# A transformer block on one Trainium2 core: the value fold in front, the score fold behind tile 0 as three fp32r products

## The chip, the cores and the metric

The kernel runs on one core of a Trainium2 chip. The metric is device time in microseconds (us), the median of the runs of a kernel. PE is TensorE, DVE is VectorE, ACT is ScalarE, POOL is GpSimd and SP is SyncE, which here only issues DMAs.

## The reference

Three layers, each with a residual; `x` is (16, 64, 512), the context (16, 1601, 512). fp32 throughout.

```python
def xattn(q, k, v, mask, gamma, beta):         # q = layernorm(x), k = v = ctx
    logits = einsum('bsd,btd->bst', q, k) / sqrt(512)
    attn = softmax(where(mask == 0, -9e15, logits))
    return layernorm(attn @ v) * gamma + beta
def attn(x, W_qkv, W_out):                     # x = layernorm(x), 64 tokens a sequence
    q, k, v = split(x @ W_qkv.T)
    return (softmax(q @ k.T / sqrt(512)) @ v) @ W_out.T
def ffn(x, router_w, expert_w1, expert_w2):    # x = layernorm(x), top 2 of 8 experts
    return sum_e gate_e * (gelu(x @ w1[e].T) @ w2[e].T)
```

## The kernel before, in words

The 1024 tokens are 8 tiles of 128 (two sequences each). One core runs five instruction streams, each written out in a fixed order and tied to the others by semaphores; there is no planner.

**Start.** The host gives the projection weights with the summed dimension on the partitions. They are turned on PE (`turn_pieces`, `turn_weights`, 128x128 transposes), copied out of PSUM, and folded in pairs: `m` is the product of query and key weights (the second layer's scores are xn m xn^T), `vo` the product of value and output weights. `fold` makes each as four 128x512 outputs of four fp32 matmuls. Each fp32 matmul shows as two PE instructions. The order is: 16 idle transposes (`keep_busy`) once the constants `cst` are there, turn wq and wk, fold `m`, tile 0's query and rest columns, tile 0's scores, turn wv, fold `vo`, tile 1's query. The result of `m` goes to `scores_w`; that of `vo` is split into two fp32r parts (`values_high` by ACT, `values_low` by DVE), for `values` multiplies fp32r parts three times (high by high, high by low, low by high).

**Turns.** In turn r (1 to 7) PE transposes the probabilities of tile r-1 (`turn_prob`), makes the scores of tile r in three blocks of 512 context rows and a rest of 65 (`scores`, L805; `rest_scores`), the second layer's keys of tile r-2 (`keys`, L861), then sums probabilities by context of tile r-1 (`sums`, L846: rest first, then three blocks), and between them the second layer's own scores, values, turned probabilities and output of tile r-2 (`own_scores` L871, `values` L879 to L881, `turn_own_probs` L887, `weigh` L893). DVE does masks and maxima (`softmax`), the low part of xn (`low_xn`, L1432), gates and ranks of the router, the next tile's query norm (`queries`), the own scores' maxima (`tops`, L1421), and the other norms. ACT does exponentials and copies. POOL turns the mask into bounds (`bounds`, L619, one 128x1601 pass a tile) and adds the bias (`add_bias`, L625).

**Loads.** All context loads go through SP's one DMA queue. The context is loaded twice, as rows (`load_ctx`, L497) and turned (`load_turned`, L510), 1 MiB a piece, into one buffer for each block: SP waits until PE has used the block of the tile before, and then issues the next. A turn loads 12 MiB, a mask and the rest rows.

**After the last turn** come the last sums, the second layer of tiles 6 and 7, the router, and the gather of expert 0's rows (`first_rows`, `hot_rows` L930), with the first weight blocks of the expert layer split into fp32r parts (`split_high` by ACT L1202, `split_low` by DVE L1501). `keep_busy` (L938) puts idle transposes where PE would wait. Then eight experts run (`up` L1066 to L1068, `down` L1095 to L1097), the second product two chunks behind the first; the last expert has two token tiles, whose rows are scaled by DVE (`gate`, L1669) and added to the output by indirect DMAs of POOL (L707).

Of the kernel before, what the change touches and what calls it, by code (L numbers as in the profile page):

```python
# [70 lines left out]
def fill_order():  # L71

    for which in ("wq", "wk", "m"):
        for n in range(KC):
            yield which, 0, n
    for kind in ("xq", "rest0", "rest1", "qr"):
        yield kind, 0, 0
    for which in ("wv", "vo"):
        for n in range(KC):
            yield which, 0, n  # L80
    for kind in ("xq", "rest0", "rest1"):
        yield kind, 1, 0
    for r in range(1, TILES):
# [20 lines left out]
def by_act(kind, t, n):  # L104
    if kind == "xn":
        return t != LAST
    return n % 2 == 0 if kind in ("wq", "wk", "m") else kind not in ("vo", "out", "qr", "logit", "rank", "pt")
# [15 lines left out]
def bank_at(kind, t, n=0):  # L123
    if kind == "wk":
        return n
# [104 lines left out]
def build(nc, x, ctx_in, ctx_turned, mask, gamma, beta, w_qkv, w_out, w_router, w1, w2, consts, acc):  # L230
# [5 lines left out]
    with ExitStack() as stack:  # L236
# [26 lines left out]
        with (nc.sbuf_tensor("before_low2", [P, 44680], F32), nc.sbuf_tensor("values_low2", [P, 2, D], F32R) as values_low2):  # L263
            pass
        high_c = sb("high_c", [P, 2, WBLK], F32R)
# [56 lines left out]
        turned_q, turned_k = [view(21504 + i * WBLK, KC, D) for i in range(2)]  # L322
        turned_v = turned_q
# [74 lines left out]
        cst_in, gb_in = sem("cst_in"), sem("gb_in")  # L398
        wq_in, wk_in = [[sem(f"{name}_in{k}") for k in range(KC)] for name in ("wq", "wk")]
        vo_high, xn_high, xn_split = sem("vo_high"), sem("xn_high"), sem("xn_split")  # L400
        wv_in, wo_in, rw_in = sem("wv_in"), sem("wo_in"), sem("rw_in")
# [88 lines left out]
        def _(sp):  # L490
# [44 lines left out]
            sp.dma_start(raw_v, w_qkv[:, 2 * WBLK:].rearrange("p (k h) -> p k h", k=KC)).then_inc(wv_in, 16)  # L535
            sp.dma_start(raw_out, w_out.rearrange("p (k h) -> p k h", k=KC)).then_inc(wo_in, 16)
# [9 lines left out]
            sp.wait_ge(filled, filled_at("vo", 0, KC - 1))  # L546
# [63 lines left out]
        def _(pool):  # L610
# [84 lines left out]
            gather(STATIC[0], 3)  # L695
            for t in range(LAST - 1, TILES):
# [45 lines left out]
        def _(pe):  # L742
# [19 lines left out]
            def turn_weights(kind, raw, hc):  # L762
                o = open_fill(kind, 0, hc)
                for k in range(KC):
                    mm = pe.transpose(o[:, k * P:(k + 1) * P], raw[:, k, hc * P:(hc + 1) * P], ident)
                mm.then_inc(filled, 1)

            def fold(kind, left, right):
# [985 lines left out]
```

## Time and profile before

| | us |
|---|---|
| median of 3 runs | 768.01 (766.83 to 769.06) |
| the profiled execution | 767.6 |
| its span | 765.9 |
| PE busy | 736.6 (96%) |
| DVE / ACT / POOL busy | 443.4 / 309.5 / 153.9 |

The span is the time from the first to the last instruction. A busy share is an average over stages with different limits; what an edit is worth is read from its own stage. In rows of the timeline an engine's idle time before an instruction stands in brackets with what ended it. A line such as L479 or L780 can be that of a helper.

### The profile page before, as it was taken

The page shows a single profiled execution, that of the slowest core. Times are in us where ns is not written, and L with a number is a line of the kernel's source. Part 1 is how long each engine was busy: PE and PEld are TensorE (multiplying, and loading weights), DVE is VectorE, ACT ScalarE, POOL GpSimd, SP SyncE. Part 2 cuts the span into 40 slices and gives each one's busy share as a digit, 9 for nine tenths or more (in the row PEclk, how much of TensorE's full clock was granted, in tenths as well). Part 3 has the DMA queues.
Part 4 walks back from the last instruction along what each step waited for, and adds up shares of the span by engine and source line. Part 5 has one row for each costly group of instructions (what it writes and reads, how often), then busy time and mean ns, then how long its engine had stood idle before and what let it go on. Part 6 is the DMA issues. An engine that isn't in the chain of part 4 may idle for free.

```text
span 765.9 us, 12386 instructions
## 1 busy us (share of the span) xinstructions
PE 736.6 (96%) x4794; PEld 560.5 (73%) x4794; DVE 443.4 (58%) x1005; ACT 309.5 (40%) x518; POOL 153.9 (20%) x162
## 2 busy tenths in 40 slices
PE   6999999999999999999999999999999999999992
PEld 5444455454545554578999999999998998888882
DVE  5243467676767664886775545555556556555620
ACT  2022212121223221335555555565555666666620
POOL 2132130404132200132310210310211230120201
PEclk9999999999999999999999999999999999999997
DMA  9999999999999999921545545655657565665302
GB/s 328 408 419 418 398 402 418 397 419 402 418 403 417 400 416 398 330 63 32 202 165 196 143 151 194 160 193 179 185 192 199 198 227 193 214 207 216 86 1 28
DMA packets 36333, 199.40 MB, mean 260 GB/s; under 512 B 4700, under 2 KB 5100, under 8 KB 15536
## 3 DMA queue, kind: packets, MB, share of 16 engines
q1 hardware_dynamic: 29912, 186.74, 63.2%
q0 software_dynamic: 4704, 9.14, 6.4%
q10 hardware_dynamic: 1656, 2.70, 1.0%
q8 instruction: 40, 0.66, 0.3%
q14 instruction: 21, 0.17, 0.1%
HBM read 188.19 MB, written 10.37 MB: 259 GB/s over the span
## 4 chain that ended last, share of the span: by engine, by line
PE 82%; DVE 11%; issue 2%; ACT 2%; DMA 1%; POOL 0%; DVEq 0%; POOLq 0%; ACTq 0%
PE ps L805 11%; PE ps L1066 8%; PE ps L1068 8%; PE ps L1067 8%; PE ps L846 7%; PE ps L1088 4%; PE ps L1089 4%; PE ps L1090 4%; PE ps L1095 4%; PE ps L1096 4%; PE ps L1097 4%; PE ps L773 4%; DVE xn_parts L1432 2%; PE ps L826 2%; PE ps L780 1%
## 5 line engine op out<-in xcount | busy, mean ns | idle before, releaser
L479 POOL TENSOR_TENSOR small<-small 128x1 f32<-128x1 f32 x64 | 24.1, 377 | 556.3 <-DVE yb_space L1669 197.4
L1068 PE MATMUL ps<-xT,low_a 128*128 128x288 f32 (+5 forms) x384 | 110.1, 287 | 0.0
L1274 ACT ACTIVATE hid<-ps 128x288 f32<-128x288 f32 (+5 forms) x128 | 50.6, 396 | 143.7 <-PE ps L1068 141.1
L1638 DVE TENSOR_TENSOR h_ring<-hid,h_ring 128x288 fp32r<-128x288 f32 (+5 forms) x128 | 55.7, 436 | 86.1 <-ACT h_ring L1279 86.0
L1501 DVE TENSOR_TENSOR low_a<-w_raw_a,high_b 128x2048 fp32r<-128x2048 f32 x32 | 73.4, 2292 | 39.2 <-ACT high_b L1202 39.2
L846 PE MATMUL ps<-arena 128*64 128x512 f32 (+1 forms) x416 | 94.1, 597 | 0.8 <-DVE arena L1401 0.8
L805 PE MATMUL ps<-arena 128*64 128x512 f32 x384 | 85.5, 596 | 0.2 <-ACT arena L1149 0.2
L1142 ACT COPY arena<-ps 128x512 f32<-128x512 f32 (+2 forms) x89 | 41.4, 525 | 100.6 <-PE ps L780 61.3
L1066 PE MATMUL ps<-xT,high_b 128*128 128x288 f32 (+5 forms) x256 | 74.9, 292 | 0.0
L1067 PE MATMUL ps<-xT,high_b 128*128 128x288 f32 (+5 forms) x256 | 73.4, 287 | 0.0
L1068 PEld LDWEIGHTS ps<-xT,low_a 128*128 128x128 f32 x384 | 72.4, 189 | 0.0
L846 PEld LDWEIGHTS ps<-arena 128*64 128x64 f32 (+1 forms) x416 | 27.9, 136 | 54.1 <-issue 51.8
L805 PEld LDWEIGHTS ps<-arena 128*64 128x64 f32 x384 | 26.3, 137 | 48.5 <-issue 47.8
L1202 ACT CAST high_b<-w_raw_a 128x2048 fp32r<-128x2048 f32 x32 | 60.8, 1904 | 0.0
L1090 PE MATMUL ps<-h_ring,low_a 128*128 128x288 f32 (+2 forms) x192 | 56.9, 296 | 0.0
L1279 ACT CAST h_ring<-hid 128x288 fp32r<-128x288 f32 (+5 forms) x128 | 53.4, 418 | 4.1
L1066 PEld LDWEIGHTS ps<-xT,high_b 128*128 128x128 f32 x256 | 48.3, 189 | 1.4
L1067 PEld LDWEIGHTS ps<-xT,high_b 128*128 128x128 f32 x256 | 48.3, 189 | 1.1
L1501 DVE TENSOR_TENSOR low_b<-w_raw_b,high_c 128x2048 fp32r<-128x2048 f32 x16 | 36.7, 2293 | 20.6 <-ACT high_c L1202 20.5
L1501 DVE TENSOR_TENSOR low_a<-w_raw_a,high_a 128x2048 fp32r<-128x2048 f32 x16 | 36.6, 2292 | 19.9 <-ACT high_a L1202 19.9
L619 POOL TENSOR_SCALAR arena<-arena 128x1601 f32<-128x1601 int32 x8 | 45.0, 5624 | 0.0
L1377 DVE SCALAR_TENSOR_TENSOR arena<-arena,ps 128x1024 f32<-128x1024 f32 (+1 forms) x16 | 15.3, 956 | 44.8 <-PE ps L805 44.8
(217 smaller groups left out, 1644.7 us busy)
## 6 DMA issues: line engine op xcount, KB each, us to landing
arena<-in_ctx_turned SPq DMA_DIRECT2D x48, 1024.0 KB, 20.4
arena<-in_ctx SPq DMA_DIRECT2D x48, 1024.0 KB, 18.7
w_raw_a<-in_w SPq DMA_DIRECT2D x48, 1024.0 KB, 4.8
w_raw_b<-in_w SPq DMA_DIRECT2D x16, 1024.0 KB, 4.8
arena<-in_mask SPq DMA_DIRECT2D x8, 800.5 KB, 22.1
tokens_x<-arena SPq DMA_DIRECT2D x11, 256.0 KB, 12.4
arena<-in_w_qkv SPq DMA_DIRECT2D x8, 256.0 KB, 4.8
out<-res SPq DMA_DIRECT2D x8, 256.0 KB, 9.2
```

Source lines behind the costliest of these rows:

```text
L619: pool.tensor_scalar(bound, mask_sb, 0, MASKED - LIMIT, ALU.is_equal, ALU.mult).then_inc(bound_ready, 1)
L805: mm = pe.matmul(bank(blk)[64 * b:64 * b + 64, :], xqT[:, k, 64 * b:64 * b + 64], ctxT[blk][:, b, k, :], start=(k == 0), stop=(k == KC - 1))
L846: mm = pe.matmul(att_ps[64 * b:64 * b + 64, :], probT[0:m, c, 64 * b:64 * b + 64], rows, start=(n == 0 and c == chunks[0]), stop=(n == NBL ...
L1066: pe.matmul(o, w_high[2 * f][:, cols], high[:, k, 0:w.width], start=(k == 0), stop=False)
L1067: pe.matmul(o, w_high[2 * f][:, cols], low[:, k, 0:w.width], start=False, stop=False)
L1068: mm = pe.matmul(o, w_low[2 * f][:, cols], high[:, k, 0:w.width], start=False, stop=(k == KC - 1))
L1090: mm = pe.matmul(o, low[:, cols], h_high[:, 0:w.width], start=False, stop=final)
L1202: act.copy(w_high[j], w_raw[j]).then_inc(w_high_ready, 1)
L1274: nc.scalar.activation(hid[:, c % 2, 0:w.width], bank(c % UP_BANKS)[:, 0:w.width], ACT.Gelu).then_inc(gelu_done, 1)
L1279: act.copy(h_ring[:, c % RING, 0, 0:w.width], hid[:, c % 2, 0:w.width]).then_inc(h_high_ready, 1)
L1501: dve.tensor_tensor(w_low[j], w_raw[j], w_high[j].bitcast(F32), ALU.subtract).then_inc(w_ready, 1)
L1638: dve.tensor_tensor(h_ring[:, c % RING, 1, 0:w.width], hid[:, c % 2, 0:w.width], h_ring[:, c % RING, 0, 0:w.width].bitcast(F32), ALU.subtr ...
```

## The change

It moves and rewrites several things at once. (1) The value and output weights are loaded, turned and folded first; the identity is loaded alone, ahead of the other constants. (2) The query and key weights are turned after that, kept as fp32r parts (high by ACT, low by DVE), and folded behind tile 0's scores and tile 1's query as 48 fp32r matmuls. (3) In the turns the second layer's own scores, values and turned probabilities of tile r-2 stand behind the rest sum alone, not behind the first block too, the output product one block earlier, and DVE takes `tops` ahead of `queries`. (4) After the last turn the low part of weight block 1 goes from DVE to POOL, and `low_xn` stands ahead of the last `attended`. (5) 23 idle transposes stand ahead of the last `ranks`, where 18 stood, and 5 more behind it. (6) The last three `down` chunks of the last expert run tile by tile.

```diff
 def fill_order():
-    for which in ("wq", "wk", "m"):
+    for which in ("wv", "vo", "wq", "wk"):
...
+    for n in range(KC):
+        yield "m", 0, n
     for r in range(1, TILES):
...
-            for raw, first, here in ((raw_q, 0, wq_in), (raw_k, KC, wk_in)):
+            for raw, of, first, here in ((raw_v, w_qkv, 2 * KC, wv_in), (raw_out, w_out, 0, wo_in), (raw_q, w_qkv, 0, wq_in),
+                                         (raw_k, w_qkv, KC, wk_in)):
                 for k in range(KC):
-                    sp.dma_start(raw[:, k, :], w_qkv[:, (first + k) * D:(first + k + 1) * D]).then_inc(here[k], 16)
-            sp.dma_start(res[:, 0:D], x[0:P, :]).then_inc(x_in, 16)
+                    sp.dma_start(raw[:, k, :], of[:, (first + k) * D:(first + k + 1) * D]).then_inc(here[k], 16)
+                if raw is raw_out:
+                    sp.dma_start(res[:, 0:D], x[0:P, :]).then_inc(x_in, 16)
...
-            sp.dma_start(raw_v, w_qkv[:, 2 * WBLK:].rearrange("p (k h) -> p k h", k=KC)).then_inc(wv_in, 16)
-            sp.dma_start(raw_out, w_out.rearrange("p (k h) -> p k h", k=KC)).then_inc(wo_in, 16)
...
-            sp.wait_ge(filled, filled_at("vo", 0, KC - 1))
+            sp.wait_ge(filled, filled_at("m", 0, KC - 1))
...
             gather(STATIC[0], 3)
+            pool.wait_ge(w_high_ready, 2)
+            pool.wait_ge(w_ready, 1)
+            carry_pool_waits(pool, own)
+            pool.tensor_tensor(w_low[1], w_raw[1], w_high[1].bitcast(F32), ALU.subtract).then_inc(w_ready, 1)
...
+            def fold_scores():
+                wait_copied(pe, "wk", 0, KC - 1)
+                for m in range(KC):
+                    o = open_fill("m", 0, m)
+                    cols = slice(m * P, (m + 1) * P)
+                    for hc in range(KC):
+                        pe.matmul(o, high_q[:, hc, cols], high_k[:, hc, :], start=(hc == 0), stop=False)
+                        pe.matmul(o, high_q[:, hc, cols], low_k[:, hc, :], start=False, stop=False)
+                        mm = pe.matmul(o, low_q[:, hc, cols], high_k[:, hc, :], start=False, stop=(hc == KC - 1))
                     mm.then_inc(filled, 1)
...
-            pe.wait_ge(cst_in, 16)
-            keep_busy(16, bank(0))
+            pe.wait_ge(id_in, 16)
+            keep_busy(6, bank(0))
+            turn_pieces("wv", raw_v, wv_in)
+            fold_values()
             turn_pieces("wq", raw_q, wq_in)
+            wait_copied(pe, "vo", 0, KC - 1)
             turn_pieces("wk", raw_k, wk_in)
-            for n in range(KC - 2, KC):
-                wait_copied(pe, "wk", 0, n)
-            fold("m", turned_q, turned_k)
             turn_query(0)
             turn_rest(0)
+            wait_copied(pe, "wq", 0, KC - 1)
             for blk in range(NBLK - 1):
                 scores(0, blk)
             rest_scores(0)
-            pe.wait_ge(wv_in, 16)
-            for hc in range(KC):
-                turn_weights("wv", raw_v, hc)
-            pe.wait_ge(wo_in, 16)
-            wait_copied(pe, "wv", 0, KC - 1)
-            fold("vo", turned_v, raw_out)
             turn_query(1)
             turn_rest(1)
+            fold_scores()
+            pe.wait_ge(cst_in, 16)
...
                 sums(r - 1, PV_ORDER[0])
-                sums(r - 1, PV_ORDER[1])
                 if runs(r - 2):
                     own_scores(r - 2)
                     values(r - 2)
                     turn_own_probs(r - 2)
-                sums(r - 1, PV_ORDER[2])
+                sums(r - 1, PV_ORDER[1])
                 if runs(r - 2):
                     weigh(r - 2)
+                sums(r - 1, PV_ORDER[2])
                 sums(r - 1, PV_ORDER[3])
...
-            keep_busy(18, open_fill("rank", LAST))
+            keep_busy(23, open_fill("rank", LAST))
             ranks(LAST)
+            wait_copied(pe, "logit", LAST)
+            keep_busy(5, bank(bank_at("logit", LAST)))
             hot_rows(LAST)
...
                     up(w, c)
-                    if c >= LAG:
+                    if w.kind == EXPERTS - 1 and c == FC - 1:
+                        for t in range(2):
+                            for late in range(FC - 1 - LAG, FC):
+                                down(w, late, t)
+                    elif c >= LAG:
                         down(w, c - LAG)
...
+                if runs(r - 2):
+                    tops(r - 2)
                 if runs(r + 1):
                     queries(r + 1)
                 if runs(r - 2):
-                    tops(r - 2)
                     copy_pt(r - 2)
                     second_norm(r - 2)
...
-            for j in range(2):
-                split_low(STATIC[0], j)
+            split_low(STATIC[0], 0)
             gates(LAST - 2)
             route_second(LAST - 2)
+            low_xn(LAST - 1)
             attended(LAST)
-            low_xn(LAST - 1)
```

## Rows read from the trace of the kernel before

**Rows 1.** Busy time by stretch: us, each engine (instructions), granted clock, DMA share, GB/s.

```profile
192.20:228.70 36.50, 36.34 (x226) 19.04 (x225) 25.00 (x87) 8.25 (x19) 9.56 (x8) 1.00 1.02 410
```

**Rows 2.** The chain that ended last, in the start: start us, us, what.

```profile
14.31 13.97 PE ps L773 x32
...
29.41 10.52 PE ps L805 x48
...
58.64 1.37 PE ps L826 x10
```

**Rows 3.** The same chain, one fp32r product of 512 columns.

```profile
290.03 0.23 PE ps L880
```

**Rows 4.** Line L529, the eight 256 KiB weight pieces.

```profile
L529 SPq DMA_DIRECT2D arena<-in_w_qkv x8: 399/432/505, 0.9 to 4.3; - x8
...
DMA to landing us min/median/max: 3.8/4.8/5.9
```

**Rows 5.** Line L510, the last turned blocks of tile 0.

```profile
L510 SPq DMA_DIRECT2D arena<-in_ctx_turned x2: 522/523/524, 8.8 to 9.4; - x2
...
DMA to landing us min/median/max: 20.3/21.6/22.8
```

**Rows 6.** Line L510, the last turned blocks of tile 3.

```profile
L510 SPq DMA_DIRECT2D arena<-in_ctx_turned x3: 1866/1880/2157, 95.4 to 99.2; - x3
...
DMA to landing us min/median/max: 27.3/27.4/28.9
```

**Rows 7.** PE's timeline: tile 3's third score block, then turn 5.

```profile
129.08 3.65 PE L805 MATMUL ps<-arena 128*64 128x512 f32 x16
...
211.65 4.51 PE L846 MATMUL ps<-arena 65*64 65x512 f32 x20
215.99 0.64 PE L871 MATMUL ps<-arena 128*64 128x64 f32 x16
...
219.76 0.33 PE L887 MATMUL ps<-cst,own_space 128*128 128x128 f32 x1 [0.16 <-ACT own_space L1183]
```

**Rows 8.** DVE's timeline in the same turn.

```profile
209.94 2.93 DVE L1432 TENSOR_TENSOR xn_parts<-arena,xn_parts 128x512 fp32r<-128x512 f32 x1
...
215.25 0.69 DVE L1350 BATCH_NORM_STATS2 small<-res 128x6 f32<-128x512 f32 x1
...
218.20 0.47 DVE L1421 TENSOR_REDUCE small<-ps 64x1 f32<-64x64 f32 x2
```

**Rows 9.** POOL's timeline in the same turn.

```profile
208.19 5.63 POOL L619 TENSOR_SCALAR arena<-arena 128x1601 f32<-128x1601 int32 x1
...
218.95 1.28 POOL L625 TENSOR_TENSOR res<-res,arena 128x512 f32<-128x512 f32 x1
```

**Rows 10.** DVE's timeline after the last turn.

```profile
312.34 4.49 DVE L1501 TENSOR_TENSOR low_a<-w_raw_a,high_a 128x2048 fp32r<-128x2048 f32 x2 [1.05 <-ACT high_a L1202]
...
332.69 0.69 DVE L1432 TENSOR_TENSOR xn_parts<-arena,xn_parts 128x512 fp32r<-128x512 f32 x1
```

**Rows 11.** POOL's timeline, the last of the three gathers.

```profile
332.97 1.17 POOL L672 DMA_INDIRECT rows_space<-tokens_x,route  x1
```

**Rows 12.** PE's timeline ahead of the expert layer.

```profile
342.77 2.21 PE L930 MATMUL ps<-arena 128*128 128x288 f32 x8
...
349.98 0.39 PE L912 MATMUL ps<-route,cst 128*128 128x8 f32 x2 [0.75 <-DVE route L1466]
...
351.25 3.66 PE L930 MATMUL ps<-arena 128*128 128x288 f32 x8 [0.66 <-DVE arena L1496]
```

**Rows 13.** Busy time by stretch, columns as in rows 1.

```profile
352.00:353.00 1.00, 1.00 (x4) 0.70 (x3) 0.90 (x5) 0.40 (x1) 0.19 (x1) 0.50 0.00 0
```

**Rows 14.** The timeline of the end.

```profile
751.60 1.46 DVE L1669 TENSOR_SCALAR yb_space<-ps,route 128x512 f32<-128x512 f32 x2 [2.24 <-PE ps L1097]
...
753.24 1.57 POOL L707 DMA_INDIRECT out<-yb_space,route  x1 [0.47 <-POOL small L479]
...
755.19 1.48 POOL L707 DMA_INDIRECT out<-yb_space,route  x1 [0.16 <-issue]
```

More of the change, by code:

```diff
@@ L106, in by_act @@
         return t != LAST
-    return n % 2 == 0 if kind in ("wq", "wk", "m") else kind not in ("vo", "out", "qr", "logit", "rank", "pt")
+    return n % 2 == 0 if kind in ("wv", "m") else kind not in ("wq", "wk", "vo", "out", "qr", "logit", "rank", "pt")
 ACTS = [by_act(kind, t, n) for kind, t, n in FILLS]
@@ L123, in bank_at @@
 def bank_at(kind, t, n=0):
[L124 removed]
+    if kind == "wq":
         return n
@@ L1093, in down @@
                     for t, (a, m) in enumerate(w.tiles):
+                        if only is not None and t != only:
+                            continue
                         o = bank(y_bank(w, t))[0:m, :]
@@ L1119, in _ @@
                     more = in_use(pe)
-            for c in range(FC - LAG, FC):
-                down(STATIC[-1], c)
             with pe.If(more > 0):
@@ L1223, in _ @@
                 act.copy(values_high[:, n, :], bank(bank_at("vo", 0, n))).then_inc(vo_high, 1)
-            copy_query(1)
-            copy_rest(1)
+            for kind, dst in (("wq", high_q), ("wk", high_k)):
+                for n in range(KC):
+                    act.wait_ge(filled, filled_at(kind, 0, n))
+                    act.copy(dst[:, n, :], bank(bank_at(kind, 0, n))).then_inc(turned_high, 1)
+            for p in range(2):
+                copy_query(p)
+                copy_rest(p)
+            exps(0)
+            for n in range(0, KC, 2):
+                copy_fill("m", 0, scores_w[:, n, :], n)
             act.wait_ge(zero_out, 16)
@@ L1511, in _ @@
             own.then_next(dve.memset(cum[0], 0.0))
+            for n in range(1, KC, 2):
+                copy_fill("wv", n, turned_v[:, n, :])
+            queries(0)
             dve.wait_ge(cst_in, 16)
@@ L1516, in _ @@
                 own.then_next(dve.memset(capacity[:, p:p + 1], float(WIDTHS[p])))
-            for kind, dst in (("wq", turned_q), ("wk", turned_k)):
-                for n in range(1, KC, 2):
-                    copy_fill(kind, n, dst[:, n, :])
-            queries(0)
-            for n in range(1, KC, 2):
-                copy_fill("m", n, scores_w[:, n, :])
-            softmax(0)
-            queries(1)
             for n in range(KC):
@@ L1528, in _ @@
                                   ).then_inc(copied[False], 1)
+            for which, (kind, high, part) in enumerate((("wq", high_q, low_q), ("wk", high_k, low_k))):
+                dve.wait_ge(filled, filled_at(kind, 0, KC - 1))
+                for n in range(KC):
+                    dve.wait_ge(turned_high, which * KC + n + 1)
+                    dve.tensor_tensor(part[:, n, :], bank(bank_at(kind, 0, n)), high[:, n, :].bitcast(F32), ALU.subtract
+                                      ).then_inc(copied[False], 1)
+            queries(1)
+            softmax(0)
+            for n in range(1, KC, 2):
+                copy_fill("m", n, scores_w[:, n, :])
             for r in range(1, TILES):
```

58 lines of the change are left out of this document (27 added, 31 removed).

## The prediction

> **What bounds the kernel now.** I read the busy times by stretch first. In a steady turn PE is busy for 36.34 of 36.50 us at full granted clock, and in the same row the DMA engines are full as well: share 1.00, 410 GB/s [rows 1]. So two resources stand near their limit at once. A turn's loads are 12 MiB of context (12.58 MB), a mask (0.82 MB), rest rows (0.27 MB) and a token store (0.26 MB), 13.9 MB; at 410 GB/s that is 34.0 us against PE's 36.5. PE sets the pace, and the queue catches up some 2.5 us a turn. What matters is how late the queue is at the beginning. I then read the chain of waits of the start: a fold is 13.97 us on PE, tile 0's scores run from 29.41 to 39.93, and turn 1 begins at 58.64 [rows 2]. No DMA stands in the chain after the first 5 us, so a reader could think that loads are hidden. The landing times say how thinly. Tile 3's last turned piece is issued at 99.2 and lands 28.9 us later, at 128.1 [rows 6]; PE takes that block at 129.08 [rows 7]. The slack is 1.0 us, the least that I found in turns 1 to 7. Third, I read one turn on PE, DVE and POOL side by side [rows 7 to 9], and last the stretch between the turns and the expert layer [rows 10 to 13] and the end [rows 14].
>
> **The start.** The score fold goes from 32 instructions in 13.97 us [rows 2] to 48 of 0.232 us (0.23 in [rows 3]), 11.15 us: 2.8 us less PE work. The new order in time: the value weights need 16 transposes, not 32, ahead of the first fold, and 6 idle ones, not 16. Pieces land from 4.7 us on, one each 0.78 us (4.7 to 10.2 for eight) [rows 4], so the value fold can begin at about 8.4 and ends 14.0 later, at 22.4. Turning wq and wk takes about 4.6, to 27.0. The parts are made by ACT and DVE bank by bank; DVE's subtraction is 0.69 each [rows 10], and tile 0's columns need the banks of wk, so I give PE 3 us of waiting, to 30.3. Here the queue speaks: all sixteen pieces now stand ahead of the context. Tile 0's last turned piece lands at 9.4 + 22.8 = 32.2 now [rows 5]; eight more pieces of 0.78 put it at 38.5. The third block would be wanted at 37.4, so scores end at 38.5 + 3.5 = 42.0. Rest, tile 1's query and rest take 1.6, the fold 11.2: turn 1 begins at 54.8, **3.8 us earlier** than 58.64.
>
> Does it last? The bytes ahead of tile 3's last piece are the same before and after, in nearly the same order, and the queue never runs empty in either. Then that piece lands at 128.1 whatever PE does, and PE, which wanted it at 129.08, can be at most 1.0 us earlier there. The value and output weights go from two 1 MiB transfers to eight small ones: eight at 0.78 are 6.3 us, 2.1 MB at 410 GB/s 5.1, so the queue may be 0 to 1.2 us later. I take 0.4, since the 0.78 is from the first microseconds, when the queue has hardly begun. That leaves **-0.6**, with -1.0 and +0.2 as bounds. If the queue is no bound, the bounds are -3.8 and, with no wait for tile 0's third block, -4.9.
>
> **The turns.** PE has the same instructions in another order. What counts is when the turned own probabilities (L887) can go. Now PE does the rest sum (4 of the 20 instructions from 211.65, 0.87 us), the first block (3.5), own scores from 215.99 to 216.56, values for 2.9, and is ready at 219.44; L887 starts at 219.76, 0.32 late [rows 7]. It waits for the exponentials, 1.56 us after DVE begins `tops` at 218.20 [rows 8]. After the change PE begins own scores at 211.65 + 0.87 = 212.5 and is ready at 216.0. DVE is at the queries at 215.25 [rows 8], which is where `tops` now stands; it can't be earlier, for low_xn takes 2.93 us there (0.69 when alone [rows 10]), beside POOL's bounds of 208.19 to 213.82 [rows 9]. So L887 starts at 215.25 + 1.56 = 216.8, 0.84 late. Taking the first block away from behind the own work costs 3.5 us of cover and `tops` gives back 2.95: **+0.5 us a turn**. That holds for turns 4, 5 and 6, +1.55. In turn 3 POOL's mask lands late, the wait is 1.5 to 1.9 us now, and the same count gives 1.35: -0.5. Turn 2 is level (-0.1), and in turn 7 POOL has no bounds, low_xn is short and nobody waits. Sum **+0.95**, between 0 (if low_xn gets in ahead of POOL) and +1.6. Behind `tops` queries delay copy_pt by 3 us, but the first block's 3.5 us cover that. The output product one block earlier gives second_norm 4 us more; in turn 7 this is the only one that shows, 0.2, counted below.
>
> **After the last turn.** DVE's two subtractions are 4.49 us [rows 10]; one goes, 2.25 us off DVE. The last `attended` waits for PE's sums anyway from about 0.8 us ahead of its start, and low_xn ahead of it takes 0.7 off a wait of PE's, so of 2.25 about 0.7 reaches PE. POOL takes the subtraction up behind the last gather (332.97 + 1.17 now [rows 11]), about 332 then, since gates are also 2.25 earlier. Its price isn't in the trace: 2048 columns at L625's 1.28/512 are 5.1 us, at L619's 5.63/1601 7.2 us [rows 9]; I take 5.1, a tensor_tensor like L625. It meets tile 7's low_xn (332.69 now, 332.0 then [rows 10]) and the routing of tile 6 on DVE. low_xn beside POOL took 2.2 us longer than alone [rows 8, 10]. Bounds: -0.7 if DVE isn't held, +0.8 if low_xn and the routing behind it are held as in rows 8. I take **-0.3**, as most of DVE's work there is on a few columns or from PSUM. The Trainium skill ("SBUF — State Buffer", "Who interferes with whom") has a DVE instruction with two SBUF inputs fully blocked by a POOL instruction that reads SBUF. By it the whole 5.1 us would be closed to low_xn, and the term would be positive; the 2.93 us in rows 8 agrees with it in kind, though there DVE was free 0.95 us ahead of POOL's shown end.
>
> **The clock.** PE idles for 0.75 us ahead of the ranks and 0.66 behind them, and the eight fp32 instructions that follow take 3.66 us; the same eight took 2.21 at 342.77 [rows 12]. The granted clock at 352 to 353 is 0.50, that is 1.2 GHz and not 2.4 [rows 13]. The new transposes fill both gaps: five at 0.12 are 0.6 of the 0.75 and 0.6 of the 0.66, and delay nothing. With the clock kept PE saves 1.45; behind it DVE's four splits of about 0.5, which start only once the gates are done, keep 0.3 of that: **-1.1** (bounds 0 and -1.5).
>
> **The end.** Of the last 18 products (0.232 each) the first tile's last is number 15 now and number 9 then. That is 1.4 us, less 0.1 for the last chunk's parts, which come later than PE asks. The first scaling moves from 751.60 to 750.3, and POOL's first DMA from 753.24 to 751.95. The second is now 1.95 behind the first, at 755.19 [rows 14]; then it needs tile 2's rows (752.3, plus 0.73 and 0.91 to the DMA) at 753.95: **-1.2** (bounds -0.9 and -1.4).
>
> **Sum.** -0.6 + 0.95 - 0.3 - 1.1 - 1.2 = -2.25 us. The profiled execution took 767.6, so 765.3 by the sum; it lies 0.4 under the median of 768.0, which gives 765.7. A measurement of this kernel can tell about 0.3%, 2.3 us: my forecast stands on that bound.
>
> **Rivals.**
> - *The queue is no bound.* For it: no DMA in the chain, slack of 4 us and more from turn 4 on. Against: 1.00 share and 1.0 us of slack in turn 3. The 3.8 us reach the end: 768.0 - 2.25 - 3.2 = 762.5. Chance 0.15.
> - *The clock falls all the same,* since 0.15 us gaps and small transposes may not count as work. 766.8. Chance 0.11.
> - *The turns pay more:* 1.6 for the turns and the queue 1.0 later, so that the front gives nothing: 768.0 - 2.25 + 0.65 + 0.6 = 767.0. Chance 0.13.
> - *The turns pay nothing:* 764.7. Chance 0.05.
> - *Slower.* POOL's subtraction holds DVE's low_xn of tile 7 to its end. At 7.2 us it ends at 339.2, low_xn at 339.9, values start 5.4 us later than 334.5 and the tail is +4.7 in place of -0.3: 770.7. It decides from a delay of PE of some 2.6 us on. For it: the stretched low_xn. Against: DVE may come first, by 0.1 us. Chance 0.10.
> - The forecast, 765.7 with its own range of 764.3 to 767.1: chance 0.46, 0.25 of it under 765.7.
>
> Faster by over 0.3%: 0.25 + 0.15 + 0.05 = 0.45. Within: 0.21 + 0.11 + 0.13 = 0.45. Slower by over 0.3%: 0.10. The range of 762.4 to 768.6 leaves out the slow case and some of the wide ends.
>
> **What would show it.** Turn 1's first transposes at about 55; a wait for a turned piece at tile 2's or tile 3's third score block, which isn't in the chain now; tile 3's third block at 128.1 to 128.9; 0.8 us ahead of L887 in turns 4 to 6; one POOL subtraction of 5 us from 332 on, and a long low_xn or routing step beside it; granted clock 1.0 at 350 to 356; the second output DMA 1.2 us nearer to the first. If tile 3's block starts at 126 or earlier, the cap by the queue was wrong, and most of my working with it.

## The result, and the profile after

The changed kernel takes **778.65 us** (median of 4 runs, 772.72 to 779.44) against 767.42 for the kernel before beside it: ratio 1.0127, 95% interval 1.0074 to 1.0181. It is slower by 11 us where I had forecast 2.25 less, and it lies outside my range. The profiled execution took 779.44 us, with a span of 777.8 (765.9 before).

Read by checkpoints, the 11.8 us between the two profiled executions arise in two places. The last turn's transposes of probabilities begin at 306.6 instead of 301.7, 4.9 late. From there to the expert layer's first product it is 62.4 us instead of 54.3 (369.0 less 306.6, 356.0 less 301.7), another 8.1. The expert layer is as long as it was, and behind it 1.3 us are won.

**The start.** First the chain of waits (start us, us, what). In the kernel before it had no DMA behind the first 5 us:

```profile
16.14 25.50 DMA arena<-in_ctx_turned
41.68 5.35 PE ps L822 x16
...
104.25 28.65 DMA arena<-in_ctx_turned
132.94 3.68 PE ps L822 x16
```

The two DMA lines answer to [rows 5, 6]. Tile 0's last turned piece lands at 41.6, not at 32.2 as before or at 38.5 as I had it, and tile 3's at 132.9, not at 128.1. PE takes them the moment they land. Its timeline in tile 0, with the idle time and its releaser in brackets:

```profile
28.46 0.63 PE L797 MATMUL ps<-cst,arena 128*128 128x128 f32 x4 [1.89 <-DVE fold_low L1549]
...
35.83 3.65 PE L822 MATMUL ps<-arena 128*64 128x512 f32 x16 [2.06 <-DMA arena<-in_ctx_turned]
41.68 1.84 PE L822 MATMUL ps<-arena 128*64 128x512 f32 x4 [2.20 <-DMA arena<-in_ctx_turned]
```

Turn 1 begins at 59.4, 0.8 later than before and 4.6 later than my 54.8. The piece's landing is 3.1 of the 4.6. Another 1.7 is TensorE's clock. Behind the waits of 2.06 and 2.20 us the granted clock is 0.50 from 41.9 to 45.3, and the third block takes 5.35 us, where such a block takes 3.65 at other times:

```profile
40.00:45.00 5.00, 3.32 (x8) 0.92 (x10) 1.22 (x1) 0.00 (x0) 0.00 (x0) 0.69 1.01 374
```

The queue never ran empty, yet it moved less. Busy time by stretch (here and above with the columns of [rows 1]) of the kernel after and then of the kernel before:

```profile
15.00:20.00 5.00, 5.00 (x13) 2.18 (x12) 2.08 (x12) 0.90 (x2) 0.00 (x0) 1.00 1.06 337
20.00:25.00 5.00, 5.00 (x28) 3.27 (x27) 1.38 (x2) 1.32 (x3) 0.00 (x0) 1.00 1.02 346
```

```profile
15.00:20.00 5.00, 5.00 (x13) 2.13 (x13) 4.72 (x9) 0.59 (x1) 5.00 (x1) 1.00 1.02 416
20.00:25.00 5.00, 5.00 (x13) 2.25 (x12) 1.41 (x2) 0.11 (x1) 0.43 (x1) 1.00 1.02 410
```

The DMA share stands above 1.00 in all four rows, but the bytes went from 416 and 410 GB/s to 337 and 346.

**The turns.** Turn 5 takes 37.00 us instead of 36.50 [rows 1], and L904, which is L887 of before, waits 0.60 instead of 0.16 [rows 7]:

```profile
197.46:234.46 37.00, 36.40 (x227) 19.05 (x225) 25.11 (x87) 8.29 (x20) 9.54 (x8) 1.00 1.01 407
```

```profile
221.13 0.33 PE L904 MATMUL ps<-cst,own_space 128*128 128x128 f32 x1 [0.60 <-ACT own_space L1203]
```

**After the last turn.** POOL, DVE and PE side by side in the profiled execution:

```profile
338.18 4.51 POOL L703 TENSOR_TENSOR low_a<-w_raw_a,high_a 128x2048 fp32r<-128x2048 f32 x1
```

```profile
337.75 4.97 DVE L1363 SCALAR_TENSOR_TENSOR small<-small 128x1 f32<-128x1 f32 x1
342.75 0.16 DVE L1365 SCALAR_TENSOR_TENSOR small<-small 128x1 f32<-128x1 f32 x1
```

```profile
334.87 3.84 PE L878 MATMUL ps<-arena 128*128 128x128 f32 x32
343.55 1.12 PE L797 MATMUL ps<-cst,arena 128*128 128x128 f32 x4 [4.84 <-DVE arena L1379]
...
347.95 0.63 PE L897 MATMUL ps<-values_low,xn_parts 128*128 128x512 f32 x1
348.38 0.63 PE L898 MATMUL ps<-values_high,xn_parts 128*128 128x512 f32 x1
```

```profile
342.30:352.30 10.00, 8.75 (x40) 7.24 (x41) 4.92 (x22) 1.59 (x6) 0.54 (x2) 0.50 0.14 52
```

A DVE step on one column, 0.22 us at other times, takes 4.97. It ends at 342.72, and POOL's subtraction at 342.69. PE, which waits for that normalization, is idle for 4.84 us. From 342.2 on, still within the idle time, its granted clock is 0.50, that is 1.2 GHz, for 10.2 us, and the value products start 0.43 us apart instead of 0.23. A further stretch at half clock, of 3.4 us at 311.5, also follows a wait of PE's (0.94 us).

The other executions of the changed kernel bear the clock out: the three at 778.5 to 779.4 us have a mean granted clock of 0.983 over the whole, the one at 772.7 has 0.990, like the profiled execution of the kernel before.

**Clock and end.** These two steps worked as forecast. The eight instructions behind the last ranks take 2.21 us, not 3.66 [rows 12], and the second output DMA starts 1.9 us behind PE's last product (765.1), where it was 3.3 [rows 14]:

```profile
365.74 2.21 PE L947 MATMUL ps<-arena 128*128 128x288 f32 x8
```

```profile
763.44 0.75 DVE L1696 TENSOR_SCALAR yb_space<-ps,route 128x512 f32<-128x512 f32 x1 [1.05 <-PE ps L1115]
...
765.08 1.57 POOL L715 DMA_INDIRECT out<-yb_space,route  x1 [0.47 <-POOL small L483]
...
767.03 1.48 POOL L715 DMA_INDIRECT out<-yb_space,route  x1 [0.16 <-issue]
```

### The profile page after: what moved, and what is told of

Same layout as the page of the kernel before. It is cut to its first block, busy times and chain, and to the rows that moved or that the text cites. A ratio compares the mean times of both kernels' runs of the same rounds, so it can differ in the third digit from the quotient of the medians.

```text
span 777.8 us, 12441 instructions
## 1 busy us (share of the span) xinstructions
PE 739.7 (95%) x4810; PEld 564.8 (73%) x4810; DVE 442.5 (57%) x1010; ACT 310.5 (40%) x520; POOL 158.5 (20%) x164
## 4 chain that ended last, share of the span: by engine, by line
PE 78%; DVE 7%; DMA 7%; SPq 4%; issue 1%; ACT 1%; POOL 0%; DVEq 0%; POOLq 0%; ACTq 0%
PE ps L863 10%; PE ps L1082 8%; PE ps L1084 8%; PE ps L1083 8%; PE ps L822 8%; DMA arena<-in_ctx_turned 7%; PE ps L1104 4%; PE ps L1105 4%; PE ps L1106 4%; PE ps L1113 4%; PE ps L1114 4%; PE ps L1115 4%; SPq L514 2%; PE ps L797 1%; DVE xn_parts L1453 1%
## 5 line engine op out<-in xcount | busy, mean ns | idle before, releaser
L863 PE MATMUL ps<-arena 128*64 128x512 f32 (+1 forms) x416 | 96.0, 606 | 1.4 <-DVE arena L1422 0.9
L822 PE MATMUL ps<-arena 128*64 128x512 f32 x384 | 87.8, 606 | 6.0 <-DMA arena<-in_ctx_turned 5.8
L1162 ACT COPY arena<-ps 128x512 f32<-128x512 f32 (+2 forms) x83 | 38.4, 519 | 97.3 <-PE ps L797 70.5
L822 PEld LDWEIGHTS ps<-arena 128*64 128x64 f32 x384 | 26.7, 138 | 56.5 <-issue 47.1
L1522 DVE TENSOR_TENSOR low_a<-w_raw_a,high_a 128x2048 fp32r<-128x2048 f32 x15 | 34.4, 2293 | 19.9 <-ACT high_a L1222 19.9
## 6 DMA issues: line engine op xcount, KB each, us to landing
tokens_x<-arena SPq DMA_DIRECT2D x11, 256.0 KB, 11.8
```

Of the source, the lines that this page charges most:

```text
L822: mm = pe.matmul(bank(blk)[64 * b:64 * b + 64, :], xqT[:, k, 64 * b:64 * b + 64], ctxT[blk][:, b, k, :], start=(k == 0), stop=(k == KC - 1))
L863: mm = pe.matmul(att_ps[64 * b:64 * b + 64, :], probT[0:m, c, 64 * b:64 * b + 64], rows, start=(n == 0 and c == chunks[0]), stop=(n == NBL ...
L1522: dve.tensor_tensor(w_low[j], w_raw[j], w_high[j].bitcast(F32), ALU.subtract).then_inc(w_ready, 1)
```

## The experiments

My theory after reading the two traces had two parts: POOL's subtraction shuts DVE out (and PE's clock pays for the idle time), and the load queue, later than I took it to be, undoes the new start. The rivals were that the new start costs PE time of its own, and that the loss after the last turn is only a follow-up of a later start and other turns. Each run stands against the kernel before timed beside it, whose median was between 767.08 and 767.74.

| part of the change | us | ratio, interval | my term |
|---|---|---|---|
| start alone | 769.29 | 1.0023, 1.0003 to 1.0044 | -0.6 |
| turns alone | 769.27 | 1.0033, 1.0021 to 1.0045 | +0.95 |
| last turn alone (POOL's subtraction, low_xn first) | 771.76 | 1.0070, 1.0047 to 1.0094 | -0.3 |
| clock and end alone | 765.51 | 0.9982, 0.9970 to 0.9994 | -2.3 |
| all but POOL's subtraction | 768.62 | 1.0024, 1.0014 to 1.0035 | |

The four parts add up to 1.08% (0.23 + 0.33 + 0.70 - 0.18), within the interval of the whole.

**All but POOL's subtraction.** DVE does both blocks again:

```diff
-            pool.tensor_tensor(w_low[1], w_raw[1], w_high[1].bitcast(F32), ALU.subtract).then_inc(w_ready, 1)
...
-            split_low(STATIC[0], 0)
+            for j in range(2):
+                split_low(STATIC[0], j)
```

> The changed kernel with one part undone: DVE makes the low part of weight block 1 again, POOL does not; low_xn stays ahead of the last attended. Theory 'port': POOL's 4.5 us subtraction held one small DVE step for 4.97 us, PE idled 4.84 us behind it and its clock was at half for the 10.24 us after; without it both go, and the time falls by 6 to 8 us to about 771.5, with no DVE step over 1.5 us in that stretch and granted clock 1.0 there. Rival 'late tail': the tail is slow because the queue and the turns made everything late, and the order around low_xn costs; then the time stays at 777 to 779 and PE still has a wait of some 5 us. In either case tile 3's third score block still starts at about 132.9, 3.9 us later than in the kernel before.

768.62 (768.02 to 769.97 over 10 runs). The one instruction is worth 10 us in the changed kernel by the medians (of 4 executions with it and 10 without), and without it the executions lie within 2 us of each other instead of 7.

**Wide pieces.** The changed kernel with wq and wk as one 1 MiB transfer each, rows of 8 KiB in place of 2 KiB:

```diff
+                if raw is raw_q or raw is raw_k:
+                    sp.dma_start(raw, of[:, first * D:(first + KC) * D].rearrange("p (k h) -> p k h", k=KC)).then_inc(here[0], 16)
+                    continue
```

> The changed kernel, but the query and key weights come as one 1 MiB transfer each (rows of 8 KiB) in place of four of 256 KiB (rows of 2 KiB). Theory 'row size': the eight extra small pieces with 2 KiB rows put the load queue 4.1 us late by the end of tile 0's loads (44.1 against 40.0) and 4.8 at tile 3; with wide rows the queue is 2 to 4 us earlier and tile 3's third score block starts at 129.5 to 131 and not at 132.9, so the time falls by 2 to 3.5 us. Rival 'order': the queue is late because of when the identity, the constants and the small loads of ACT's queue mix with SP's; then landing times move by less than 1 us and the time by less than 1.

770.56 (767.90 to 775.83), POOL's subtraction still in it, so the median says little of the queue. The page's line on packets of the changed kernel and of this run (36333 packets in the kernel before):

```profile
DMA packets 37341, 199.40 MB, mean 256 GB/s; under 512 B 4812, under 2 KB 5468, under 8 KB 16800
```

```profile
DMA packets 36478, 199.40 MB, mean 260 GB/s; under 512 B 4717, under 2 KB 5373, under 8 KB 15681
```

A good yardstick of the queue's lateness is the landing of the slots' write, which stands behind all the first loads: 40.0 in the kernel before, 44.1 after, 41.5 here. It varies from one execution to the next, though. In the ten traces with the old start it is 39.7 to 41.2, in the five with the new start and small pieces 42.2 to 44.1, and with wide pieces 41.5 and 43.0 (the second from a run further on). So wide pieces give back some 1 us on the average of so few, and most of the lateness has another cause. Tile 3's third block is at 130.3 here, as the theory had it, but at 131.3 and 133.3 in two further runs with wide pieces, and at 131.4 to 132.9 with small ones.

**Clock and end alone**, on the kernel before (the transposes and the order of the last 18 products, as in the diff of the change).

> The kernel before with two parts of the change alone: the 5 + 5 more idle transposes around the last ranks, and the last expert's last down chunks tile by tile. My sum gave -1.1 and -1.2: 765.1 against 767.4, ratio 0.997. The granted clock should stay 1.0 at 352 to 355, and the second output DMA should start 1.2 us nearer to the end of PE's work. Rival: a clock that falls all the same leaves -1.2 (0.9984); if the end is set by the DMAs' landing and not by their issue, less.

765.51 against 767.08. The profiled execution shows 2.8 less (764.84 against 767.6), no half clock ahead of the expert layer, and its first product 1.5 earlier. The timed median keeps 1.6 of it. The traces of all the runs show most of the reason: in the ten without this edit, the eight instructions behind the last ranks take 2.92 to 3.90 us in five and 2.21 in the other five; in the nine with it they always take 2.21. So the loss was there in half of these executions only, and 3.66 against 2.21, from which I priced the edit, was one of those. The mean of the ten is 2.80, which makes it worth 0.6 us and not 1.45.

**Turns alone**, PE's and DVE's order as in the change, on the kernel before.

> The kernel before with the order of the turns alone: own scores, values and turned probabilities behind the rest sum, the output product one block earlier, tops ahead of queries. Theory: 0.5 us a turn lost in turns 4 to 6, 0.5 won in turn 3, in sum +1.0 us (ratio 1.0013), and turns of 36.96 us in place of 36.50. Rival: the earlier second_norm wins that back after the last turn, ratio 1.000; or the changed meeting of DVE and POOL costs more, 1.003.

769.27: dearer than my +0.95, by the interval +1.6 to +3.5. The turns are 36.96 us, 0.46 longer, as in the whole.

**The start alone.** Value fold first, score fold in fp32r parts, everything behind as before.

> The kernel before with the new start alone: value fold first, score fold as 48 products of fp32r parts behind tile 0's scores; turns, last turn, clock and end as before. Queue theory: turn 1 begins some 3 us earlier (about 56), but tile 3's third score block comes 2 to 3 us later than before's 129.1, and the time is 1.5 to 2.5 us over the kernel before (about +0.3%). Rival (the delay of the start is not the queue's but that of the parts made by ACT and DVE): turn 1 begins at 58 or later. My prediction on record had -0.6 for this part.

769.29. Turn 1 begins at 56.5, 2.2 earlier than in the kernel before, and tile 3's third score block at 132.4, 3.4 later. Between them PE waits above all 2.99 us for plain context and 0.66 for a turned piece:

```profile
80.44 1.94 PE L859 MATMUL ps<-arena 128*64 128x512 f32 x8 [2.99 <-DMA arena<-in_ctx]
```

So the score fold's gain was there, and the queue took more than all of it. The granted clock is 1.00 from the start to turn 3 in this trace, so here the loss isn't the clock's. The clock can come on top, though: of the eight traces of kernels with the new start and the full queue, seven have one or two stretches of about 3.4 us or more at half clock before 90 us, and none of the nine with the old start and the full queue has one. What these stretches cost in the end was not measured.

**The same with the queue relieved.** If the queue takes it, then taking load off the queue must give it back. Both kernels get the same edit, which halves tile 1's turned context:

```diff
+                    n = KC // 2 if p == 1 else KC
-                    sp.dma_start(ctxT[blk][:, b, :, :], ctx_turned[2 * p + b, :, LOADED_TURNED - 1 - blk, :, :]
+                    sp.dma_start(ctxT[blk][:, b, 0:n, :], ctx_turned[2 * p + b, :, LOADED_TURNED - 1 - blk, 0:n, :]
```

> The kernel before, but tile 1's turned context is loaded by half (3.1 MB less ahead of everything from tile 1 on; what stands in the buffers is used in place of the other half, so the numbers that it computes are others; PE's work is the same). It is the base line for the next run. Both theories: within 0.5 us of the kernel before, since no PE wait for a load of more than 0.6 us is in its trace.

> The new start alone, with tile 1's turned context loaded by half, as in the run beside it (the same loads left out). Queue theory: with 7 us of transfers taken away the gain at turn 1 reaches the end, so the time is 2.5 to 3.5 us UNDER that of the relieved kernel before, where the start alone without relief is 1.5 to 2.5 over. Rival (the new start costs PE time of its own, or clock): the relieved pair differs by about as much as the unrelieved one, +1.5 to +2.5.

The kernel before went to 765.64 (0.9971, 0.9957 to 0.9986), the one with the new start to 764.57 (0.9953, 0.9933 to 0.9973). The new start costs 1.6 us with the full queue and saves 1.1 with the relieved one. The saving by itself isn't clear of the noise, for the two intervals overlap. The swing of 2.7 us between the pairs is: I estimate its standard error from the single executions at 0.9. The rival, which excludes a swing, is out. But I had expected a saving of 2.5 to 3.5, and the trace tells why it is less. At tile 3's third block the new start is 1.1 ahead (127.0 against 128.1). In the same turn L901 (L887 of before) begins at 144.5 in both, behind a wait of 1.26 us with the new start and of none in the other:

```profile
144.48 0.33 PE L901 MATMUL ps<-cst,own_space 128*128 128x128 f32 x1 [1.26 <-ACT own_space L1197]
```

POOL's bounds of this turn, which need a mask from the same queue, run from 133.0 to 138.6 in both (the mask lands at 132.7 with the new start and POOL takes it at once; in the other it lands at 131.0 and POOL waits for DVE), and DVE's low_xn beside them ends at 137.6 in both, however early it began. It takes 4.09 us in the one and 2.92 in the other:

```profile
132.98 5.62 POOL L624 TENSOR_SCALAR arena<-arena 128x1601 f32<-128x1601 int32 x1
```

```profile
133.55 4.09 DVE L1447 TENSOR_TENSOR xn_parts<-arena,xn_parts 128x512 fp32r<-128x512 f32 x1
```

That is a second way from the queue to PE: mask, POOL's bounds, DVE, tops, exponentials, L887. The relieved kernel before, too, was to be level and gained 2.1 us, although no wait of PE's over 0.6 us for a load stood in its trace: its L887 in turn 3 lost its wait of 1.48, and the mask, on which POOL had waited, lands at 131.0 instead of 135.0.

**The last turn alone.** POOL's subtraction and low_xn ahead of the last attended, on the kernel before.

> The kernel before with the last turn's part of the change alone: POOL makes the second static block's low parts (one subtraction of 2048 columns), DVE's low_xn ahead of the last attended. Theory (DVE's small steps of the router, with operands in SBUF, are shut out for as long as POOL's instruction runs, and PE's idle time then brings its clock down): 3 to 10 us slower, single times spread over 5 us and more, since it depends on which of the two comes first; in the trace one small DVE instruction of 2.5 to 5 us beside POOL's. Rival (the loss after the last turn comes only together with the later start and the new order of the turns): within 1 us of the kernel before. My prediction had -0.3.

771.76 (768.96 to 777.70). The single executions are of two kinds: three at 777.3 to 777.7 with a mean granted clock of 0.983 or 0.984, the others at 769.0 to 772.8 with 0.986 to 0.992. The profiled execution is the fastest of them (768.96), and even there DVE's step ends with POOL's, at 337.57 and 337.54:

```profile
332.96 4.58 POOL L699 TENSOR_TENSOR low_a<-w_raw_a,high_a 128x2048 fp32r<-128x2048 f32 x1
```

```profile
334.40 3.17 DVE L1460 SCALAR_TENSOR_TENSOR route<-route,cst 128x8 f32<-128x8 f32 x1
```

The rival, that the loss needs the rest of the change, is out. The edit has low_xn in front as well; on another version that alone changed nothing (further on), so the loss is POOL's subtraction.

**A quarter of it.** POOL makes 512 of the 2048 columns. In the first form DVE's own share stood ahead of the first block and waited 2.85 us for ACT's parts, a fault of my edit; the second form keeps the old order.

```diff
-            pool.tensor_tensor(w_low[1], w_raw[1], w_high[1].bitcast(F32), ALU.subtract).then_inc(w_ready, 1)
+            pool.tensor_tensor(w_low[1][:, 0:BLK], w_raw[1][:, 0:BLK], w_high[1][:, 0:BLK].bitcast(F32), ALU.subtract).then_inc(w_ready, 1)
```

> The same with POOL doing 512 of the 2048 columns (DVE the other 1536, ahead of it, where it did all of them before). Theory of the hold: the longest that DVE can be held falls from 4.5 us to about 1.2, PE's idle time stays under a microsecond more than before, and the time is within 1 us of the kernel before (it may even be under it by 0.7, what DVE saves). Rival (what costs is the handing over, POOL's start and the semaphores between the engines, and not the length): as slow as the full one.

> The kernel before with POOL making 512 of the 2048 columns and low_xn first, and DVE's share in the old order (the first block as soon as its high parts are there). Theory (the time is lost by DVE being shut out for the length of one POOL instruction, 1.27 us here): within 1 us of the kernel before, and the runs within 3 us of each other. Rival (it is the meeting of the two engines, whatever its length, or the handing over): some 2 us slower and spread over 8, as the first quarter run.

The first form took 769.66 (ratio 1.0026, 1.0002 to 1.0050; 765.82 to 774.62), 2.3 over the kernel before where I had expected 1 at most, the second 768.02 (1.0015, 0.9995 to 1.0035). POOL's instruction is 1.28 us in it. Eleven of the twelve runs are between 764.9 and 769.7, and one is 774.57. So handing the work over costs little: 4.4 us for 2048 columns, 0.6 for 512, which is within the noise. Neither trace has a held step, however. In the second form POOL's 1.28 us run from 334.32, DVE waits for PE from 334.29 on and then, at 335.10, takes up a step that reads PSUM. So the short instruction met nothing, and what a meeting with it costs isn't shown. The spread did not go away quite as expected; the one at 774.57 has a mean granted clock of 0.984, the others 0.989 and over.

**Whole, but in four instructions.**

```diff
+            for q in range(4):
+                cols = slice(q * BLK, (q + 1) * BLK)
+                part = pool.tensor_tensor(w_low[1][:, cols], w_raw[1][:, cols], w_high[1][:, cols].bitcast(F32), ALU.subtract)
+            part.then_inc(w_ready, 1)
```

> The kernel before with POOL's whole subtraction, low_xn first, but as four instructions of 512 columns. If DVE's step gets in between two POOL instructions, no DVE step is longer than about 1.4 us, several are long, and the time is 0 to 2 us over the kernel before, with runs of 777 gone. If POOL keeps what they share over all four, there is a step of 2.5 to 5 us as with one instruction, and the time is again near 771 with runs of 777.

771.40 (1.0065, 1.0043 to 1.0087), as dear as in one. DVE, whose step is shown as beginning 0.09 us ahead of the first of the four, did not get in between them:

```profile
333.24 4.99 POOL L701 TENSOR_TENSOR low_a<-w_raw_a,high_a 128x512 fp32r<-128x512 f32 x4
```

```profile
332.55 0.69 DVE L1439 TENSOR_TENSOR xn_parts<-arena,xn_parts 128x512 fp32r<-128x512 f32 x1
333.15 5.25 DVE L1568 CAST arena<-arena 128x288 f32<-128x288 int32 x1
338.44 0.48 DVE L1428 TENSOR_REDUCE small<-ps 64x1 f32<-64x64 f32 x2
```

**The changed kernel once more**, a single execution with its profile.

> The changed kernel as it is, for a second look. Theory: a DVE step of up to 5 us beside POOL's subtraction, PE idle for some 5 us behind it and its clock at half for 10 us, if the time is near 779; if it is near 772, the long step is shorter or falls where PE still has work, and the clock stays up.

771.67. The held step is another one, a comparison on 8 columns of 2.57 us, ending at 341.26 with POOL's 341.23:

```profile
338.69 2.57 DVE L1477 SCALAR_TENSOR_TENSOR route<-route,cst 128x8 f32<-128x8 f32 x1
```

PE still had its value products to do and was idle for 2.12 us only, and half clock lasted 3.4 us instead of 10. So which of DVE's steps POOL meets, and what PE has left to do then, most likely makes the difference between 772 and 779; it rests on one trace of each kind.

**Better versions.** On DVE tops go ahead of the queries, PE keeps the turn of before, and clock and end are as changed:

```diff
+                if runs(r - 2):
+                    tops(r - 2)
                 if runs(r + 1):
                     queries(r + 1)
                 if runs(r - 2):
-                    tops(r - 2)
                     copy_pt(r - 2)
```

> The kernel before with three things of the change alone: on DVE tops go ahead of the queries (PE's order of the turn stays that of before), the transposes around the last ranks, and the end with the first tile's products first. The transposes and the end alone gave 765.5 against 767.1. Theory of the turns (the order on DVE gives, the order on PE takes cover away): L887's wait of 0.3 us goes in each of five turns, and the time is 1 to 2 us under those two alone, 764. Rival: the queries now delay what is behind them, and nothing is gained or 0.5 lost: 765.5 to 766.

**762.86** (0.9939, 0.9917 to 0.9960), 4.9 us under the kernel before, 1.6 of it the clock and the end, and so some 3.3 DVE's order. In the trace it is 2.7 us less from L887 of turn 2 to that of turn 7. The steady turn is 36.12 us, with PE busy for all of it:

```profile
190.50:226.62 36.12, 36.12 (x226) 19.02 (x225) 24.95 (x87) 8.23 (x20) 9.55 (x8) 1.00 1.02 410
```

```profile
216.55 0.40 PE L881 MATMUL ps<-values_high,xn_parts 128*128 128x512 f32 x1
216.78 0.27 PE L887 MATMUL ps<-cst,own_space 128*128 128x128 f32 x1
```

> The best kernel so far (tops first on DVE, transposes around the ranks, the end; 762.9 against 767.7), and low_xn ahead of the last attended. Theory: it takes 0.7 off a wait of PE's after the last turn, 762.2. Rival: attended is on the path as well and the two cancel, 762.9.

> The changed kernel without POOL's subtraction and with PE's order in the turn as before, and wq and wk loaded as 1 MiB each. So it is the best kernel with the new start added (and low_xn first). Queue theory: the new start costs 0.5 to 1.5 us with the wide loads, so 763.3 to 764.5. Rival (with shorter turns PE is closer to the queue, and a late queue costs more): 765 and over.

low_xn first gives 762.78 (0.9928, 0.9909 to 0.9947), the same. With the new start and wide loads added it is 764.26 (0.9951, 0.9932 to 0.9970), 1.5 more, timed beside it, as the queue theory had it.

**ACT's loads later.** In the kernels with the new start, x's second block, gamma, beta and the router's weights go from 9 us on, beside the pieces of wq and wk. On the start alone, and on the version just before this, they were moved:

```diff
-            act.dma_start(res[:, D:2 * D], x[P:2 * P, :]).then_inc(x1_in, 16)
...
                     act.copy(dst[:, n, :], bank(bank_at(kind, 0, n))).then_inc(turned_high, 1)
+            act.dma_start(res[:, D:2 * D], x[P:2 * P, :]).then_inc(x1_in, 16)
...
             for p in range(2):
                 copy_query(p)
```

> The new start alone, with ACT's four loads (x's second block, gamma, beta, router weights) issued behind its copies of the turned wk, at about 27 us, instead of at 9 us. Theory (two queues of small rows beside each other cost rate, and ACT's loads take their place ahead of tile 0's context): tile 0's last turned piece lands some 3 us earlier, at about 38, PE's wait for it goes, tile 3's third block comes at 130 or before, and the time is 1 to 2 us under the start alone (769.3), level with the kernel before. Rival (the bytes are the same and only their order changes; the lateness is from the wv and wo pieces ahead): tile 0 gains, but the slots' write again lands at 42 to 44, tile 3's block stays at 131.4 to 132.9, and the time is 769.

> The same move of ACT's loads in the kernel with everything but POOL's subtraction and PE's order in the turn, wq and wk in wide pieces, which took 764.26. Theory: 762 to 763, level with the best version (762.8) or just under it. Rival: 764.3 again, the place of ACT's loads is not what makes the queue late.

769.04 (1.0026, 1.0011 to 1.0041) and 764.59 (0.9961, 0.9948 to 0.9975): nothing gained, and the slots' write lands at 42.2 and 42.8 again. Tile 0's last turned piece lands at 39.6 in the first, where I expected 38, and tile 3's third block begins at 132.7 and 133.3, where I expected 130 in the first. The rival holds: the place of ACT's loads isn't it.

## Why the prediction was wrong

**After the last turn: the step that failed most.** I took -0.3 on the ground that most of DVE's work there is on a few columns. Alone the step costs 4.4 us, and in the whole kernel some 10. My slower rival named the mechanism and put +4.7 on it, with a chance of 0.10. What I got wrong in it was twofold. I looked only at whether low_xn, 512 columns wide, would meet POOL, and gave DVE a chance to come first by 0.1 us. But a narrow step is held just as long, and in normalization and routing narrow steps of 0.15 to 0.25 us stand one behind the other, so that POOL met a step of DVE's in all five traces in which it did the 2048 columns (a narrow one in four, a cast of 288 columns in the fifth). I had also read [rows 8] as if DVE were free 0.95 us ahead of POOL's end. It wasn't: the cast right behind low_xn, 0.17 us at other times, took 1.05 and ended with POOL.

```profile
212.79 1.05 DVE L1472 CAST route<-route 128x2 int32<-128x2 f32 x1
```

And I did not count the clock, which the idle time brought down. POOL's own time was nearer than I thought, 4.5 where I took 5.1. The Trainium skill ("SBUF — State Buffer", "Who interferes with whom") says that issue order and not the shape of an operation decides who blocks; I had quoted the block and passed over this sentence. As to the shape the traces agree with it: 128 by 1 was held 4.97 us. As to the order they don't bear it out in every case. In the run of the last turn alone POOL's subtraction begins first (332.96 against 334.40), but in the changed kernel the held step is shown as beginning 0.43 us ahead of it (337.75 against 338.18).

**The front.** That the queue caps the start was right, and so was the fold: 48 products from 48.38 to 59.39, 11.0 us where I had 11.15. DVE's wait was 1.9 where I allowed 3 (27.0 and 3 are 30.0, not 30.3, which changes nothing, as the landing at 38.5 came after). What failed is the queue's lateness of 0.4 us: -0.6 became +1.6 alone. I checked that the queue never runs empty and that the bytes ahead are the same; both hold, but it carried 337 and 346 GB/s there instead of 416 and 410. Tile 3's third block comes at 131.4 to 132.9 in the four traces of this start with the loads as changed, at 128.5 to 130.2 in the nine of the old start with a full queue. Neither the size of the pieces (some 1 us) nor the place of ACT's loads (nothing) accounts for it. It is there by 44 us already, 2 to 4 us, and what makes the queue slower in the first 25 us with the new order of loads stays open. I had also looked only at the turned pieces. In the start-only run the longest wait is for plain context, and the relieved pair shows a third path through the mask.

**The turns.** The mechanism was right: tops at 219.57, 22.0 us into the turn where I had 22.1 (25.0 before), L904 waiting 0.60 for my 0.84, and 0.46 us a turn for my 0.5. The term was +0.95 and measured +2.2 alone. The profiled execution of that run shows 0.8 more at the expert layer and 1.0 in all; what else the median holds is open. In tops' place I had weighed both edits together. The DVE edit by itself is a gain of 0.38 us a turn (36.12), and with PE's new order it is a loss of 0.46. PE's order was never run without DVE's, so what it costs is a difference.

**Clock and end.** The sizes hold against the one trace before: 1.45 us less for the eight instructions, and some 1.4 (I had 1.2) at the end. Together -2.8 in one profiled execution, -1.6 by the medians, and -2.3 predicted. The clock's term was too large, since the half clock comes in about half of the executions only.

**Rivals.** "The queue is no bound" is refuted by the relieved pair and by two DMAs in the chain. "The clock falls all the same" is refuted behind the ranks (full clock there in all nine traces with the edit) and came true elsewhere, behind POOL's hold and in the start.

## What to carry to other kernels

Before work moves to POOL, look at what DVE does in that time: a chain of narrow steps on the critical path can pay for nearly the whole length of POOL's instruction (4.97 us on one column beside 4.51, 3.17 on eight beside 4.58), and cutting POOL's instruction up doesn't help when its parts follow each other. A queue that is busy all the time can still be slower: compare GB/s, not the share, and follow each kind of load to its user, the mask through POOL and DVE too. When an edit reorders two engines, try each order alone; here DVE's half was worth some 3 us, and with PE's half the sum was a loss of 2. Before pricing an edit from a stretch at half clock, look in several executions whether it is always there.

## What the runs showed of the hardware that I had not expected

- Four POOL instructions in a row held one DVE instruction for all four, 5.25 us against 4.99, and that instruction, a cast of 288 columns with a single input in SBUF, takes 0.37 us at other times (the quarter runs).
- POOL's bounds (5.62 us shown) let one DVE instruction through before their shown end and hold the next to it: low_xn ends at 137.6, 0.96 us ahead of the bounds (138.60), and the cast on two columns behind it takes 1.05 us and ends at 138.62. Behind a single subtraction of 2048 columns DVE ended 0.03 to 0.04 us after POOL.
- PE's idle time of 4.84 us went with 10.2 us at half clock, while 3.4 us followed on an idle time of 2.12 and on one of 0.94. The wait behind the last ranks, 0.65 to 0.66 us in the ten traces without the added transposes, went with half clock in five of them and with full clock in five.
- Taking 3.1 MB off the load queue made the kernel before 2.1 us faster, with no wait of PE's over 0.6 us for a load in its trace.
